# Six layer norms of a fused audio tower: the centred values come from one matrix product and stay in PSUM

## The reference, cut to what matters

```python
m = jnp.mean(x, axis=-1, keepdims=True)
v = jnp.var(x, axis=-1, keepdims=True)
return (x - m) / jnp.sqrt(v + eps)
```

## Time and profile before

| | |
|---|---|
| median of 3 runs | 375.73 us (375.6 to 379.77) |
| the profiled execution | 377.35 us |
| its span, first to last instruction | 375.4 us |
| granted TensorE clock, mean over the span | 0.945 of full |
| TensorE matmul busy | 323.4 us (86%) |
| VectorE busy | 219.9 us (59%) |
| ScalarE busy | 197.5 us (53%) |
| GpSimd busy | 142.3 us (38%) |

### The profile page before, as it was taken

One profiled execution on the slowest core, in us unless ns is written; L12 is line 12 of the kernel. 1 busy time (PEld: TensorE's weight loads), 2 busy tenths in 40 slices (PEclk: granted clock), 3 DMA queues, 4 the chain that ended last, 5 costly groups with the idle time before them and its releaser, 6 DMA issues.

```text
span 375.4 us, 11768 instructions
## 1 busy us (share of the span) xinstructions
PE 323.4 (86%) x4888; PEld 219.3 (58%) x4888; DVE 219.9 (59%) x446; ACT 197.5 (53%) x382; POOL 142.3 (38%) x146
## 2 busy tenths in 40 slices
PE   4999899999997799999939893778787869979996
PEld 2446567666865534334314452668787869934684
DVE  4469987787456743232488489995566711376102
ACT  1584564445456366867674789257200095464631
POOL 9107999804000046456322403679980000031000
PEclk9999999999996899999977999599999999987999
DMA  7722222210011222211000000000000000000002
GB/s 253 299 59 64 60 63 61 59 58 16 2 44 57 61 59 58 64 57 56 3 0 0 0 0 2 0 3 4 3 6 3 5 3 3 5 0 0 2 3 80
DMA packets 20556, 14.80 MB, mean 39 GB/s; under 512 B 2328, under 2 KB 19352, under 8 KB 20376
## 3 DMA queue, kind: packets, MB, share of 16 engines
q1 hardware_dynamic: 20504, 14.07, 11.9%
HBM read 13.32 MB, written 0.74 MB: 37 GB/s over the span
## 4 chain that ended last, share of the span: by engine, by line
PE 63%; DVE 21%; ACT 8%; POOL 5%; issue 3%; DVEq 0%; POOLq 0%
PE PS L788 58%; PE PS L851 4%; DVE arena L735 3%; DVE arena L591 2%; DVE arena L574 2%; POOL arena L339 2%; ACT arena L376 1%; ACT arena L373 1%; POOL arena L335 1%; ACT arena L488 1%; POOL arena L334 1%; DVE arena L738 1%; DVE PS L523 1%; ACT arena L492 1%; ACT arena L368 1%
## 5 line engine op out<-in xcount | busy, mean ns | idle before, releaser
L788 PE MATMUL PS<-arena,K 128*128 128x360 f32 (+2 forms) x576 | 149.1, 512 | 20.1 <-DVE arena L591 6.4
L788 PE MATMUL PS<-arena 128*45 128x45 f32 (+5 forms) x3392 | 120.0, 223 | 23.2 <-ACT arena L468 11.2
L788 PEld LDWEIGHTS PS<-arena 128*45 128x45 f32 (+3 forms) x3392 | 102.7, 129 | 41.1 <-issue 25.1
L788 PEld LDWEIGHTS PS<-arena,K 128*128 128x128 f32 (+2 forms) x576 | 71.3, 183 | 79.8 <-issue 21.5
L316 POOL TENSOR_TENSOR arena<-arena 128x360 f32<-128x360 f32 x32 | 30.0, 948 | 63.2 <-DVE arena L697 62.5
L697 DVE TENSOR_TENSOR arena<-PS,arena 128x360 f32<-128x360 f32 x32 | 17.1, 533 | 33.7 <-ACT arena L422 33.7
L400 ACT COPY arena<-PS 128x360 f32<-128x360 f32 x32 | 14.8, 467 | 24.2 <-PE PS L851 24.2
L418 ACT ACTIVATE arena<-PS,K 128x720 f32<-128x720 f32 x32 | 25.0, 860 | 2.5 <-PE PS L788 2.5
L344 POOL TENSOR_TENSOR arena<-arena 128x360 f32<-128x360 f32 x4 | 4.4, 1111 | 55.8 <-DVE arena L582 55.8
L305 POOL TENSOR_TENSOR arena<-arena,K 128x360 f32<-128x360 f32 x32 | 24.1, 797 | 0.0
L488 ACT ACTIVATE arena<-arena,K 128x360 f32<-128x360 f32 x8 | 4.3, 589 | 34.9 <-DVE arena L770 34.9
(11 more groups left out here) (126 smaller groups left out, 408.5 us busy)
## 6 DMA issues: line engine op xcount, KB each, us to landing
WG<-wr SPq DMA_DIRECT2D x64, 64.0 KB, 1.9
arena<-wr SPq DMA_DIRECT2D x64, 64.0 KB, 1.8
arena<-xT SPq DMA_DIRECT2D x4, 368.0 KB, 4.5
K<-consts SPq DMA_DIRECT2D x1, 1171.0 KB, 13.0
K<-consts SPq DMA_DIRECT2D x1, 852.0 KB, 11.2
out<-arena SPq DMA_DIRECT2D x4, 180.0 KB, 1.9
K<-consts SPq DMA_DIRECT2D x1, 510.0 KB, 9.0
K<-consts SPq DMA_DIRECT2D x1, 352.0 KB, 9.7
```

What stands on the lines that cost most here:

```text
L788: return nc.tensor.matmul(o, l, r, start=start, stop=stop)
```

## The change

The constant `cent` is new: the identity minus the matrix `mean`, 128 x 128 fp32, in group 0 of the constants. In the `mean` step TensorE multiplies the source by `cent` in place of `mean`, so `bank(c, 0)` receives the centred value itself. The VectorE subtraction of the step and its semaphore are gone. ScalarE squares straight from `bank(c, 0)`. In the `var` step VectorE takes the centred value from `bank(c, 0)` and the other factor from SBUF. The first slot of `NORM_SLOTS` is still where `lt` and `gn` write their result. The order of the steps is the same.

```diff
-    [("tokA", 64), ("tokB", 64), ("mean", 128), ("vecs", 36)],
+    [("tokA", 64), ("tokB", 64), ("mean", 128), ("cent", 128), ("vecs", 36)],
...
                 elif name == "mean":
-                    xc, sq = NORM_SLOTS[LNS[i]]
+                    sq = NORM_SLOTS[LNS[i]][1]
                     act.wait_ge(sem["ln_xc"], n)
-                    s.activation(a(c, sq), a(c, xc), ACT.Square).then_inc(sem["ln_sq"], 1)
+                    s.activation(a(c, sq), bank(c, 0), ACT.Square).then_inc(sem["ln_sq"], 1)
...
-                if name == "mean":
-                    src = slot(9) if LNS[i] == "gn" else H_
-                    dve.wait_ge(sem["ln_mean"], n)
-                    v.tensor_tensor(a(c, NORM_SLOTS[LNS[i]][0]), a(c, src), bank(c, 0),
-                                    ALU.subtract).then_inc(sem["ln_xc"], 1)
-                elif name == "var":
-                    xc, sq = NORM_SLOTS[LNS[i]]
-                    dst = xc if LNS[i] in ("lt", "gn") else N_
+                if name == "var":
+                    out_, sq = NORM_SLOTS[LNS[i]]
+                    dst = out_ if LNS[i] in ("lt", "gn") else N_
                     dve.wait_ge(sem["ln_rs"], n)
-                    v.tensor_tensor(a(c, dst), a(c, xc), a(c, sq), ALU.mult).then_inc(sem["ln_out"], 1)
+                    v.tensor_tensor(a(c, dst), bank(c, 0), a(c, sq), ALU.mult).then_inc(sem["ln_out"], 1)
...
-                    mm(bank(c, 0), k("mean"), a(c, src)).then_inc(sem["ln_mean"], 1)
+                    mm(bank(c, 0), k("cent"), a(c, src)).then_inc(sem["ln_xc"], 1)
...
     z["mean"] = ((q[:, None] // 64) == (q[None, :] // 64)) / float(D)
+    z["cent"] = np.eye(128) - z["mean"]
```

More of the change, by code:

```diff
@@ L68 @@
 r_id r_oh wsI wsum
-tok_mm tok_y h0 ln_mean ln_xc ln_sq ln_var ln_log ln_rs ln_out
+tok_mm tok_y h0 ln_xc ln_sq ln_var ln_log ln_rs ln_out
 q_mm q_mul q_sum q_bd k_mm k_mul k_sum kx v_mm vd s_mm s_max s_sub s_exp pt_mm pt_ev pv_mm o_rec att
```

## The result

The changed kernel takes 373.95 us (median of 20 runs, 371.46 to 377.11), the kernel before 377.29 (20 runs, 375.52 to 379.77). The ratio is 0.9916, 95% interval 0.9891 to 0.9942, so about 3.2 us faster (2.2 to 4.1). Medians and spans in this document are over all runs, while the ratios leave out the few executions more than 1.5% above the fastest of their kernel (here the one at 377.11). The forecast was 3.6 us less, to 372.1 us. The median before, of three runs when the prediction was made, was 375.73; with 20 it is 1.6 us higher, near the profiled execution.

A forecast was written before the change was run, and what follows sets the result against it. TensorE product work was taken to bound the kernel (63% of the chain), with norms the short stretches off it. Gains 1.48 + 0.64 + 0.58 + 0.69 + 0.2, rounded 3.6 us, from 375.73 gave 372.1 us; range 369.3 to 375.6.

The forecast's parts named there:

- The four norms from ready inputs: In `lt`, `l2`, `gn`, `l4` the first logarithm comes 0.37 us earlier each, held by the variance product; together 1.48 us.
- `l1`: Norm whose subtractions queue behind gamma and beta on VectorE: first logarithm at 23.44 instead of 24.08, gain 0.64 us.
- `l3`: Norm whose last chunk comes late from GpSimd: its square moves up, the table load hides the variance product; gain 0.58 us.
- The gates behind `gn`: GpSimd's gate steps behind `gn` no longer held up by the multiplication: 0.23 us for each of three chunks, 0.69 us.
- The mixes behind `l3`: Behind `l3`, GpSimd's pair overlaps a VectorE multiplication once; that overlap ends 0.2 us sooner.
- Reading PSUM in the last multiplication: Each norm's final multiplication with one operand from PSUM: between -0.003 and +0.002 us each, taken as zero.
- The larger load: First load 64 KB larger, 0.18 us, covered by VectorE's clearing of PSUM: cost 0, or 0.2 us if uncovered.
- The second rival: Clock drop behind `gn` stays out, so products of `ro` and `l4` save 1.7 us: 370.4 us; chance 0.14.
- The slower rival: A long low-clock stretch of 10.2 us covers the gapless routed stage behind `l4`: 1.5 us slower, 377.2; chance 0.06.

The follow-up runs named there:

- the other order: Changed kernel with steps mean 0, mean 1, var 0, mean 2, var 1, mean 3, var 2, var 3 in all six norms: 369.96 us, ratio to before 0.9805.
- the copy: Changed kernel, but VectorE copies the centred value from PSUM to SBUF and the last multiplication reads SBUF: 376.0 us, ratio to before 0.9959.
- the opposite half: Kernel before, VectorE still subtracting but into PSUM in place; square and last multiplication read PSUM: 375.11 us, ratio 0.9944.
- the second profile of the changed kernel: Changed kernel run again, nothing edited, on the chip of three other experiments: 373.01 us median of 6, ratio to before 0.9904.
- extra products: Changed kernel plus six unread TensorE products behind `gn`, ahead of the output products: 373.44 us, ratio to before 0.9847.
- both halves above: The copy (changed kernel, multiplication from SBUF again), ratio 0.9959, and the opposite half (kernel before, subtraction into PSUM), ratio 0.9944.

## Why the prediction was right

The gain was forecast at 3.6 us and came out at 3.2, and its terms were right one by one. The time, 372.1 forecast and 373.95 measured, is less good, for the reason at the end of this section.

- **The four norms from ready inputs** (forecast 0.37 each): 0.37 in `gn` by the start of the first square, 0.34 in `l2` by the table, and `lt` 0.37 once the 0.26 us is taken off by which this execution started its centring products earlier (12.82, before 13.08). In `l4` the first logarithm now comes 0.61 us behind the start of the last square, as in `gn` (0.60). The reason given, that the variance product is late next, was tested by the other order and held.
- **`l1`** (0.64): 22.84 - 21.32 = 1.52 from the last centring product to the logarithm, before 24.08 - 21.93 = 2.15; 0.63.
- **`l3`** (0.58): 0.60.
- **The gates behind `gn`** (0.69) gave 0.65, and the operand's place was shown to be the cause in both directions, by the copy and by the opposite half. **The mixes behind `l3`** (0.2) gave 0.18. There the evidence is thinner: with the multiplication from PSUM, line 437 starts 17.06 and 17.07 us behind the first logarithm of `l3` (changed kernel, opposite half) against 17.24 before, but with the copy, where the instructions fall differently, it is 17.37 and GpSimd's pair doesn't get slower again.
- **Reading PSUM in the last multiplication** cost nothing, 530 against 531 ns. The 65 ns worked out from the Trainium skill's figures ("VectorE: DVE Perf Modes", the section on the TRN2 errata) don't show for this instruction with two inputs.
- **The larger load** cost nothing in the one execution that had it alone.

By the marks the change's own part is 0.37 + 0.61 + 0.34 + 0.60 + 0.18 + 0.37 + 0.65 + 0.36 = 3.5 us, against 3.6 in the forecast and 3.2 by the ratio. In `lt`, `gn` and `l4` that takes the way through the norm itself in place of the table's entry. The rest of the profile's 5.0 us came mainly from where the clock was low, and that is luck: with the clock as in the second profile of the changed kernel the same instructions took 1.33 us more from `l2` to `l3` and 1.14 less from `gn` to `l4`. The second rival came half true by the same luck, and with a warning: the low stretch behind `gn` was half as long, and cost more, since it lay on the gapless products. The rival put 1.7 us on a stretch of 7 us; one of 3.4 us cost 1.68. The slower rival's mechanism exists, but on 3.4 us and not on 10. What the prediction took too lightly is the spread: a start from three runs hid that the median of the kernel before lies 1.6 us higher, which is most of the 1.85 us by which the forecast time was missed.

## What to carry to other kernels

An instruction taken out of a chain is worth the distance to what is late next, not its duration: find the product or load that queues behind the same engine's other chunks, and try another order of the steps together with the change. A step that leaves an engine's queue can make an order cheap that was ruinous before (here 3 us of gain against 28 of loss). Where VectorE and GpSimd alternate, look at which VectorE instructions have both tensors in SBUF; here one operand left in PSUM took 0.23 us off each GpSimd step beside them.

## What the runs showed of the hardware

GpSimd's 128 x 360 fp32 step takes 1.17 us when a VectorE instruction with two SBUF tensors starts just ahead of it, and 0.94 when that one reads a tensor from PSUM, whether or not VectorE does more in all (both halves above). Behind `gn` the clock fell to the lower of its two levels after a pause of TensorE of 2.13 us and, in the changed kernel, after one of 1.58 us followed by sparse products (330.49 on); in the profiles where extra products or the other order left no pause above 0.55 us there, it didn't. The stretch of 3.4 us cost 1.68 us there, half its length.
